# A mixture of eight experts: all experts on all tokens, or tokens sorted by expert through DRAM

## The reference

```python
logits = xf @ Wg.T                       # 2048 x 8
idx = jnp.argmax(logits, axis=-1)
out = jnp.zeros_like(xf)                 # 2048 x 128
for e in range(E):                       # E = 8
    m = (idx == e)[:, None].astype(xf.dtype)
    h = jax.nn.relu(xf @ W1[e] + b1[e])  # 128 -> 512
    out = out + m * (h @ W2[e] + b2[e])  # 512 -> 128
```

## Time and profile before

| | |
|---|---|
| median of 3 runs (range) | 1242.61 us (1237.24 to 1242.72) |
| profiled execution, its own time | 1243.85 us |
| its span, first to last instruction | 1242.2 us |
| granted clock of PE over the span | 0.801 of 2.4 GHz |
| PE busy | 881.1 us (71%) |
| DVE, ACT, POOL busy | 743.5, 411.8, 103.0 us |
| experts' block, first to last product on PE | 533.9 to 743.4 us |

### The profile page before, as it was taken

One profiled execution on the slowest core, in us unless ns is written; L12 is line 12 of the kernel. 1 busy time (PEld: TensorE's weight loads), 2 busy tenths in 40 slices (PEclk: granted clock), 3 DMA queues, 4 the chain that ended last, 5 costly groups with the idle time before them and its releaser, 6 DMA issues. The chain is left out here.

```text
span 1242.2 us, 17736 instructions
## 1 busy us (share of the span) xinstructions
PE 881.1 (71%) x6628; PEld 748.9 (60%) x6628; DVE 743.5 (60%) x1601; ACT 411.8 (33%) x722; POOL 103.0 (8%) x61
## 2 busy tenths in 40 slices
PE   4957698809724002589999994799999995427984
PEld 2437698805422002478989883588888885226864
DVE  3259996494667997321526356526767764576375
ACT  2326252204301001143544431224555552205552
POOL 0021030000004781000000000000000002000000
PEclk9977588658766556689999996558999998668987
DMA  6001200210001000000000002000000000000000
GB/s 162 0 0 23 47 2 2 117 83 1 0 0 53 0 0 0 1 1 1 1 0 0 0 0 96 0 1 2 1 1 0 2 2 1 0 0 1 1 0 34
DMA packets 17799, 19.65 MB, mean 16 GB/s; under 512 B 16592, under 2 KB 16720, under 8 KB 16976
## 3 DMA queue, kind: packets, MB, share of 16 engines
q1 hardware_dynamic: 17744, 18.90, 4.9%
HBM read 17.76 MB, written 1.15 MB: 15 GB/s over the span
## 5 line engine op out<-in xcount | busy, mean ns | idle before, releaser
L1633 PEld LDWEIGHTS PS<-VXT,PT 128*128 128x128 f32 x1024 | 129.6, 205 | 17.5 <-issue 13.3
L1633 PE MATMUL PS<-VXT,PT 128*128 128x73 f32 (+1 forms) x1024 | 136.8, 290 | 4.0 <-ACT PT L1656 4.0
L1274 ACT ACTIVATE HID<-PS,PB 128x512 f32<-128x512 f32 x128 | 87.3, 689 | 100.9 <-PE PS L1247 100.8
L1743 DVE TENSOR_REDUCE MX<-PS 128x2 f32<-128x512 f32 x128 | 81.6, 685 | 64.0 <-PE PS L1598 63.5
L1254 PEld LDWEIGHTS PS<-PB,HID 128*128 128x128 f32 x1024 | 118.6, 192 | 2.2
L1254 PE MATMUL PS<-PB,HID 128*128 128x128 f32 x1024 | 118.8, 275 | 0.0
L1342 DVE SCALAR_TENSOR_TENSOR OB<-PS,MS,OB 128x128 f32 (+1 forms) x128 | 36.1, 345 | 129.8 <-PE PS L1254 129.8
L1656 ACT ACTIVATE PT<-PS 128x512 f32<-128x512 f32 x128 | 68.6, 596 | 54.1 <-PE PS L1603 54.1
L1595 PE MATMUL PS<-Q,KZ 32*128 32x256 f32 x512 | 84.8, 430 | 2.0 <-ACT KZ L1412 2.0
L1598 PE MATMUL PS<-KZ,Q 32*128 32x256 f32 x512 | 82.2, 464 | 4.9 <-DVEq L113 3.1
L273 PE MATMUL PS<-PB,NRM 128*128 128x128 f32 x80 | 17.9, 417 | 88.1 <-DVE NRM L257 52.5
(11 more groups left out here) (354 smaller groups left out, 1963.9 us busy)
## 6 DMA issues: line engine op xcount, KB each, us to landing
PB<-in_pb SPq DMA_DIRECT2D x1, 5016.0 KB, 16.2
PB<-in_pd SPq DMA_DIRECT2D x1, 2888.0 KB, 9.6
X<-in_x SPq DMA_DIRECT2D x2, 1024.0 KB, 4.8
X<-fir_rows SPq DMA_DIRECT2D x2, 1024.0 KB, 6.7
TR<-fir_rows SPq DMA_DIRECT2D x2, 1024.0 KB, 8.8
PA<-in_pa SPq DMA_DIRECT2D x1, 1731.0 KB, 8.6
PC<-in_pc SPq DMA_DIRECT2D x1, 1560.0 KB, 6.8
out_x<-X SPq DMA_DIRECT2D x2, 512.0 KB, 2.7
```

The costliest lines, as they stand in the source:

```text
L1274: nc.scalar.activation(HID[:, e % 2, c, :], PS[:, n % 8, :], ACT.Relu, bias=pb("b1")[:, at:at + 1]).then_inc(moe_act, 1)
L1633: last = nc.tensor.matmul(PS[:, UM.bank(n), col:col + VX], PT[:, k % 4, c, f * P:(f + 1) * P], v, start=(c == 0), stop=(c == 1))
L1743: nc.vector.tensor_reduce(MX[:, :, k], PS[:, UP_.bank(n), :].rearrange("p (f q) -> p f q", f=2), AX.X, ALU.max, negate=True).then_inc(p_dv ...
```

## The change

The experts are no longer applied to all tokens. The tokens are sorted by expert into slots of 128 (a block). Each expert's tokens begin at a new block, so that 16 + 8 - 1 = 23 blocks (`SLOTS`) always suffice, and each block has a single expert.

- The place of each token is worked out from `MS`: a product with a triangular matrix (`AFTER`) gives the tokens of the same expert ahead of it in its tile, a product with ones (`ONES`) the number in each tile; DVE adds these up over the tiles and the experts into `PLACE` (a row number), and finds each block's expert (`OWNER`).
- POOL scatters the rows of `NRM` by 16 indirect DMAs into the DRAM tensor `by_expert`, which SP has cleared in the first layer. SP loads it back as `XB` in six groups (`GROUPS`).
- For each of the 23 blocks, in a pipeline written out by hand (`events`, handed round by `Flow`): PE transposes the tokens (per group), makes one fp32 up product of 512 columns whose W1 is addressed by a register, loaded from `OWNER`; DVE adds b1 by the same register into `H1`; PE transposes it four times; ACT takes the Relu; PE makes the four down products, W2 by register; DVE copies the result to `EO`. SP stores it in six groups in `expert_out`.
- When all is stored, POOL gathers by 16 indirect DMAs into `MO`, and DVE adds this to `OB`.
- The norms of all four quarters follow, in waves: quarter g's norm k is in wave g + k. The subtraction and scaling is moved from DVE to ACT.
- The split of W1 and of the tokens goes. b1 is spread over the partitions once (`B1B`, by 32 products with a column of the identity).

```diff
+by_expert = nc.dram_tensor("by_expert", (SLOTS * P, D), F32, kind="Internal").ap()   # and expert_out
 # first layer, SP, behind the last toeplitz load
+sp.wait_ge(slot_zero, 1)
+sp.dma_start(slots(by_expert), ZERO.unsqueeze(1).to_broadcast([P, SLOTS, D])).then_inc(slots_clear, 16)
 # block L1060, SP
 sp.dma_start(PC[:, :], pc_in).then_inc(loadC, 16)
+sp.wait_ge(r_sorted, 16 * NT)
+for n, group in enumerate(GROUPS):
+    own = slice(group.start, group.stop)
+    sp.dma_start(XB[:, own, :], slots(by_expert)[:, own, :]).then_inc(xb_in[n], 16)
 # POOL
-for e in range(E):
-    cols = slice(e * DF, (e + 1) * DF)
-    G.link(nc.gpsimd.tensor_copy(W1H[:, cols], pb("w1")[:, cols]))
-    nc.gpsimd.tensor_tensor(W1L[:, cols], pb("w1")[:, cols], W1H[:, cols], ALU.subtract).then_inc(w1_split, 1)
+nc.gpsimd.memset(ONES[:, :], 1.0).then_inc(r_const, 1)
+nc.gpsimd.memset(AFTER[:, :], -1.0).then_inc(r_const, 1)
...
+nc.gpsimd.iota(IOTA[:, 0:16], [[P, 16]], base=0, channel_multiplier=0).then_inc(r_const, 1)
...
+pool.wait_ge(slots_clear, 16)
 # (the attention's products as before, then)
+pool.wait_ge(r_place, 1)
+for t in range(NT):
+    nc.gpsimd.indirect_dma_start(by_expert, bass.IndirectOffsetOnAxis(ap=PLACE[:, t:t + 1], axis=0),
+                                 NRM[:, t, :], None).then_inc(r_sorted, 16)
 # PE, after the QKV products
+nc.tensor.transpose(PS[0:4 * E, 7, 0:P], pb("b1"), ident).then_inc(b1_full, 1)
+(32 products that spread b1 over the partitions, taken by ACT into B1B)
 # PE, after the choice
+nc.tensor.matmul(PS[:, 5, 0:P], AFTER[:, :], chosen, start=True, stop=True)
+nc.tensor.matmul(PS[:, 5, P:2 * P], ONES[:, :], chosen, start=True, stop=True).then_inc(r_rank, 1)
 # DVE, after the choice
+V.link(nc.vector.tensor_copy(SCAN[:, 0, 8:8 + NT, :], by_tile(PS[:, 5, P:2 * P])))
+for n, far in enumerate((1, 2, 4, 8)):
+    V.link(nc.vector.tensor_tensor(new[:, 8:8 + NT, :], old[:, 8:8 + NT, :], old[:, 8 - far:8 - far + NT, :], ALU.add))
...
+V.link(nc.vector.tensor_reduce(SR[:, 0:NT], rank, AX.X, ALU.add))
+nc.vector.tensor_copy(PLACE[:, :], SR[:, 0:NT]).then_inc(r_place, 1)
...
+nc.vector.tensor_scalar(OWNER[:, :], SR[:, 16:40], float(E - 1), None, ALU.min).then_inc(r_owner, 1)
 # the experts' block
+events = [(("x", 0), "A", [6]), (("x", 1), "A", [7])]
+for j in range(SLOTS + 2):
+    if j < SLOTS:
+        events.append((("up", j), "V", [j % 2]))
+    if j % 4 == 3 and j // 4 + 2 < len(GROUPS):
+        events.append((("x", j // 4 + 2), "A", [6 + j // 4 % 2]))
+    if 1 <= j <= SLOTS:
+        events.append((("turn", j - 1), "A", [2 + (j - 1) % 2]))
+    if j >= 2:
+        events.append((("down", j - 2), "V", [4 + j % 2]))
 # PE
+expert[j] = pe.value_load(OWNER[0:1, j:j + 1], min_val=0, max_val=E - 1)
+last = nc.tensor.matmul(bank, XBT[:, j * P:(j + 1) * P], pb("w1")[:, bass.ds(expert[j] * DF, DF)],
+                        start=True, stop=True)
...
+for c in range(4):
+    last = nc.tensor.matmul(bank[:, 0:D], HT[:, j % 2, c, :], pb("w2")[:, bass.ds(expert[j] * DF + c * P, P)],
+                            start=(c == 0), stop=(c == 3))
 # SP, per group:  expert_out <- EO, when its last block is copied
 # POOL
+pool.wait_ge(moe_stored, 16 * len(GROUPS))
+for t in range(NT):
+    nc.gpsimd.indirect_dma_start(MO[:, t, :], None, expert_out,
+        bass.IndirectOffsetOnAxis(ap=PLACE[:, t:t + 1], axis=0)).then_inc(moe_back[t // 4], 16)
 # DVE, behind the blocks; ACT goes through the same waves
+for w in range(NORMS + NG):
+    if w >= 1:
+        for k, g in WAVES[w - 1]:
+            middle(k, g)          # reciprocal, and minus mean times it
+        for k, g in WAVES[w - 1]:
+            end(k, g)             # waits for ACT's four tiles; gain and shift, or the sum with x
+            if k + 1 < NORMS:
+                begin(k + 1, g)   # statistics, aggregation, variance plus epsilon
+    if w < NG:
+        begin(0, w)               # waits for the quarter's four gathers
```

More of the change, by code:

```diff
@@ L37 @@
 FIR_ROW = 192
+SLOTS = NT + E - 1
+GROUPS = [range(n, min(n + 4, SLOTS)) for n in range(0, SLOTS, 4)]
 PACK_A = [("ident", 128), ("low", 128), ("upp", 128), ("incl", 128), ("wqkv", 384), ("cwb", 1536),
@@ new lines, in _ @@
+                    V.link(nc.vector.tensor_reduce(BLK[:, 0, 4:4 + E], own_f(E, NT), AX.X, ALU.add))
+                    for n, far in enumerate((1, 2, 4)):
+                        old, new = BLK[:, (0, 1, 2)[n], :], BLK[:, (1, 2, 1)[n], :]
+                        V.link(nc.vector.tensor_tensor(new[:, 4:4 + E], old[:, 4:4 + E], old[:, 4 - far:4 - far + E],
+                                                       ALU.add))
+                    ends = BLK[:, 1, 4:4 + E]
+                    V.link(nc.vector.tensor_tensor(BLK[:, 2, 4:4 + E], ends, BLK[:, 0, 4:4 + E], ALU.subtract))
@@ L1219, in build @@
[L1219 to L1233 removed]
+            XBT = sbuf(sb, "XBT", [P, SLOTS * P])
+            H1 = sbuf(sb, "H1", [P, 2, DF])
+            HT = sbuf(sb, "HT", [P, 2, 4, P])
@@ new lines, in build, with _ @@
+            F = Flow(moe_full, {"A": moe_act, "V": moe_dve}, events)
+            with nc.Block() as block:
+                @block.sync
+                def _(sp):
+                    for group in GROUPS:
+                        own = slice(group.start, group.stop)
+                        F.wait_taken(sp, ("down", group.stop - 1))
+                        sp.dma_start(slots(expert_out)[:, own, :], EO[:, own, :]).then_inc(moe_stored, 16)
+                @block.gpsimd
+                def _(pool):
+                    pool.wait_ge(moe_stored, 16 * len(GROUPS))
+                    for t in range(NT):
+                        nc.gpsimd.indirect_dma_start(
+                            MO[:, t, :], None, expert_out,
+                            bass.IndirectOffsetOnAxis(ap=PLACE[:, t:t + 1], axis=0)).then_inc(moe_back[t // 4], 16)
@@ L1298, in begin @@
+                    def begin(k, g):
+                        own = slice(4 * g, 4 * g + 4)
+                        src = (OB, NRM, X, OB)[k]
+                        if k == 0:
+                            dve.wait_ge(moe_back[g], 16 * 4)
+                            V.link(nc.vector.tensor_tensor(OB[:, own, :], OB[:, own, :], MO[:, own, :], ALU.add))
+                        for t in range(4 * g, 4 * g + 4):
                             last = nc.vector.bn_stats(STAT[:, t, :], src[:, t, :])
@@ L1360, in _ @@
-                    for step in range(NORMS + 1):
-                        post(NG - 1, step)
+                            V.link(nc.vector.tensor_tensor(NRM[:, own, :], NRM[:, own, :], rows(gain, 4), ALU.mult))
+                            V.link(nc.vector.tensor_tensor(NRM[:, own, :], NRM[:, own, :], rows(shift, 4), ALU.add))
+                    dve.wait_ge(loadC, 16)
+                    for w in range(NORMS + NG):
+                        if w >= 1:
+                            for k, g in WAVES[w - 1]:
+                                middle(k, g)
+                            for k, g in WAVES[w - 1]:
+                                end(k, g)
[3 more added lines that the diff above has]
+                            begin(0, w)
```

281 lines of the change are left out of this document (167 added, 114 removed).

## The result

The changed kernel takes 1128.24 us (median of 4 runs, 1126.98 to 1128.72), the kernel before took 1242.66 us beside it (4 runs, 1237.24 to 1245.56). The ratio is 0.9085, with a 95% interval of 0.9056 to 0.9114: 114 us or 9% faster. The forecast was 1161 us.

A forecast was written before the change was run, and what follows sets the result against it. TensorE alone was taken to bound the experts' block. There 168.7 us replace 243.4 (-74.7), with -7.2 before it -81.9; 1243.85 less that and less 1.24 gave 1161 us, range 1125 to 1218.

The forecast's parts named there:

- the rival of the cheap DMA: Scatter and first gathers: an indirect DMA takes 0.4 us of POOL, total 1131 to 1137 us; chance 0.12.
- the sum: All terms as forecast, from the choice of experts to the next block and before: 1145 to 1185 us; chance 0.52.
- Before the experts: First norm of the block: without POOL's W1 split, DVE's 16 instructions fall from 11.40 to 4.19 us, -7.2 us.
- Scatter: POOL's 16 indirect DMAs before the experts: 1.6 us each and 1.6 for the last landing, +27.2 us.
- the dear one: Scatter and gathers: an indirect DMA takes 3.6 us of POOL, total 1218 us; chance 0.04.
- the one in which POOL waits for each transfer: Scatter and gathers: 5.2 us for each indirect DMA, total 1270 us, slower than before; chance 0.07.
- Experts: The loop of 23 blocks: 2.6 us per block, 59.8, with start 5 and drain 3, +67.8 us.
- low-clock-or-registers rival: Experts' loop: PE at 1.2 GHz throughout, 1216 us, or bare register loads of 1.6 us, 1198 us; chance 0.12.
- Start and drain: Ends of the experts' loop: first transposes to add at the low clock 5 us, drain 3 us.
- Norms: After the gathers: all four quarters bare, 47 us of DVE work and 8 us of waits, +55 us.
- Contention of DVE and POOL: Norms beside the gathers: writing descriptors holds up DVE, +17 us, 1178 us; chance 0.12. Other direction: 1161 to 1169 us.

The follow-up runs named there:

- e1: The kernel before, with POOL's split of W1 begun only when DVE's first norm of the block is done: 1233.56 us, ratio 0.9932.
- e2: The changed kernel with POOL's 16 instructions of the W1 split put back, their results unused: 1137.92 us, ratio 0.9163.
- e5: The changed kernel with each of the 16 scatters issued twice, the second into rows nobody reads: 1147.97 us, ratio 0.9246.
- e3: The changed kernel with constants (expert j mod 8) in place of PE's and DVE's register loads: 1140.29 us, ratio 0.9157.
- e4: The changed kernel with the norms' subtraction and scaling back on DVE: 1136.92 us, ratio 0.9149.
- e10: The changed kernel with each wave's first-quarter scaling shared by DVE and ACT, and SP's loads moved behind the barrier: 1137.32 us, ratio 0.9149.
- e13: e10 with seven additions of 128 x 512 on DVE behind the last wave: 1131.34 us, ratio 0.9093.
- e8: The kernel before, with 14 unused products on PE beside its last norms: four times 1225.15, 1225.14, 1244.96 and 1247.63 us.
- e12: The changed kernel, unedited, profiled a second time: 1136.53 us, ratio 0.9109.
- e11: The kernel before, unedited, profiled a second time: a single time of 1237.05 us.
- e6: The changed kernel with 14 unused fp32 products on PE beside the last norms: 1141.58 us, ratio 0.9204.

## Why the prediction was right, and where it was off

The direction, the mechanism and the range held; the time is 33 us under the forecast, and only 3 us above the lower end of the range. By the spans, 97.1 us came from the edited parts where 81.9 were forecast (15.2 too little), and 18.5 from parts that the forecast left as they were. That the time lies so near the rival of the cheap DMA (1131 to 1137) is chance: an issue costs three times what that rival had. Without the 18.5 us the time would be some 1147 us (an estimate from the spans), within the 1145 to 1185 of the sum.

**Before the experts, -7.2.** Measured 7.1 to 7.3, shown by e1 and e2. It was read from two rows with one instruction under different neighbours.

**Scatter, the first mis-sized term: 21.5, not 27.2.** The step was to take a whole transfer's 1.6 us as POOL's time for an issue. It is 1.27 us, which e5 confirms by doubling. SP's load goes out 2.27 us after the last issue begins, so the landing adds little. The rival of a cheap DMA (0.4 us) fell, and so did the dear one and the one in which POOL waits for each transfer. The Trainium skill's 2.15 us for a DMA of this queue (DMA: Bandwidth & Descriptors, Anatomy of one DMA — SWDGE (gpsimd) path) is near the 2.5 us that the DMA view of the changed kernel gives as median from issue to landing, and these overlap, one every 1.27 us: it was right not to charge them to POOL one by one.

**Experts, the larger miss: 57.3, not 67.8.** The step was 2.6 us for a block, with its share of the token transposes; it is 2.26. Of the 0.34 us, 0.2 were for addresses from registers, which e3 shows to cost nothing in the running loop; that half of the low-clock-or-registers rival fell. The other 0.14 are in the products (2.26 instead of 2.4: the transposes 0.51 instead of 0.60, the four down products 0.89 instead of 0.96). 59.8 less 52.0 for 23 blocks is 7.8 of the 10.5 us. Start and drain, forecast at 8, took the other 57.3 - 52.0 = 5.3 us. The low clock, the rival's other half, held for the first 6 us only.

**Norms: 55.8, forecast 55,** though by two errors that cancel. DVE's work with the small gaps in it is 45.4 us (43.0 and 2.4) instead of 47, its waits for ACT 10.4 instead of 8. The estimate of 0.30 us for an activation of 128 columns was too low: four take 1.65 us, 0.41 each. e4 prices the other choice (6.9 us more in D), e10 a better one (4.9 less).

**Contention of DVE and POOL.** It was a rival for the gathers, and it did not come: DVE's passes keep 0.68 to 0.69 us beside them. The forecast said that the trace shows the two holding each other up; e1 shows that in the norm only DVE was held up. In the gathers it is POOL that waits, and little. Three of the 16 issues begin while DVE adds or multiplies 128 x 512 elements (607.50, 610.23 and 614.32 us). They take 1.17, 1.29 and 1.40 us instead of 0.95, and each ends 0.82 us after DVE's instruction does. All issues in the ten sorting kernels that begin inside such a pass do so, to 0.02 us; those that begin beside DVE's statistics (603.75 us) or just before a pass (602.50) keep 0.94 to 0.95. Together that is 1.0 us, and DVE asks for the last quarter only 11 us after its landing. The Trainium skill (SBUF — State Buffer, SBUF: two separate sides) has such a lock, held for the whole of a DVE instruction that has two inputs in SBUF, against a GpSimd one that reads SBUF; the trace agrees with it here. The forecast weighed it at one pass of 0.69 us for each of twelve gathers, 8 us: only the rest of a pass is lost, and only where an issue begins in one.

**What was left out.** That parts with unchanged instructions could change their time. The 12.6 us of E hang on PE's clock in the third layer, which rises 51 us after the load instead of 84. They aren't due to the work that the change saves: e10, 5 us shorter in D, loses them and more, e13 has them back, and e8 has them without any sorting. The -7.7 of B and +1.8 of A lie ahead of every edit but the clearing of the slots and vary from run to run; e12 has +9.7 and +5.4 against e11 there, and gains 94.7 us in the span instead of 115.6. What decides them wasn't settled, nor why the clock rises earlier in one kernel than in another; one profile of most kernels is too little for that. A scatter with fewer, wider indirect DMAs wasn't tried.

## What to carry to other kernels

Sorting by expert paid although its serial parts (places, scatter, loads, gather: 40 us) and the bared norms (56 us) took back most of a stretch of 243 us; the scatter's length is the number of issues on POOL, 1.27 us each, and not the transfers. Before such a rewrite, look at whether one engine's instruction has two durations in the trace: the 7 us here were to be had by one wait. Where totals jump by 10 us and more, cut the span at fixed marks and compare the edited stretch, which repeated to 0.1 us.

## What was not expected of the hardware

- An indirect DMA of 128 rows of 512 bytes holds POOL for 0.96 us and 0.30 us pass to the next; the scatter's first took 1.20, the gathers' first, after more idleness, 0.98.
- An issue of a gather that begins while DVE adds or multiplies two SBUF tensors of 128 x 512 ends 0.82 us after that instruction, however much of it was left (0.35 to 0.58 us in the changed kernel); beside DVE's statistics it takes its usual 0.95 us.
- Loading a register from SBUF and addressing by it cost 0.8 us at the start of the loop and nothing in the 18 running steps that were compared (40.63 us with and without).
- Five us less idleness of PE ahead of a layer went with 15 us more for that layer and the next (D and E 149.0 and 482.8 against 153.9 and 467.7), and giving the five us back undid it (154.0 and 467.5), in one profile of each edited kernel. Products run meanwhile cost 10 us of E in the changed kernel (e6) and gave 13 in the one before (e8).
